# Every step of a four-layer attention kernel placed anew, with plans and PSUM banks of their own for the first two and the last two groups

## Chip, cores and metric

The kernel runs on one core of one Trainium2 chip. The metric is the device time of one launch in microseconds, the median of three runs.

## What is computed

A batch of 128 sequences, 64 tokens of 128 features, goes through four layers, each of which also reads a context tensor of the same shape. In short:

```python
x = L0(x, ctx)   # 16 heads of 8: q/k/v projections, causal scores (key < query), softmax, Wo,
                 # + x, layernorm, relu FFN 128-512-128, + , layernorm
x = L1(x, ctx)   # 16 heads of 8, no mask, softmax(q k / sqrt(8)) v, Wo, + x, gelu FFN, +
x = L2(x, ctx)   # vision = mean over ctx tokens; agreement with the text projection gives a softmax
                 # over tokens; gate = sigmoid(...); x + gate * weighted vision; layernorm
x = L3(x, ctx)   # RMS norm, 16 heads of 64: softmax(q k) v, wo, + x
```

No sequence depends on another one.

## The kernel before

The batch is cut into 16 groups of 8 sequences (512 tokens). For each group the kernel does the same 129 steps on TensorE (PE), and others on ScalarE (ACT), VectorE (DVE) and GpSimd (POOL). A step is a few instructions that belong together. The names that count here, with the layer l, the half u of a group, and the tile t:

- `xT`, `cT` transpose the input and the context; `q`, `k`, `v` project; `S.l.u` makes the scores of four sequences for layers 0 and 1, `shift.l.u.t` subtracts the row maximum in PSUM, `PT.l.u.t` transposes the probabilities, `O.l.u` multiplies them by the values, `o.l` is the output projection. Between them stand `max`, `sum`, `ctx`, `attout` on DVE, `exp`, `probT` on ACT, and `norm` on POOL (L895), which divides by the sum.
- `lnT.n`, `lnF.n` are the transposes into and out of a layernorm, with `stats` and `z` on DVE and `rstd` on POOL between; `h.l.j`, `f.l.j` are the FFN, with `relu` or `gelu` on ACT between.
- `vis`, `gv`, `ag`, `gp` belong to layer 2, with `amax`, `gate_pre`, `vis_route`, `fuse` on DVE, `route`, `gate` on ACT.
- `k3.p`, `v3.b`, `q3.p` project for layer 3 (three matmuls each), evicted on ACT as `K3`, `V3`, `Q3`; `rows` spreads the RMS factors; `S3.m`, `shift3`, `PT3`, `O3.m`, `out3.m` are its attention in four pairs of sequences, with `norm3` on POOL (L915).

`S`, `O`, `S3` and `O3` are the tiled steps: they use parts of the array (32x64, 64x32, 64x64 rows by columns), and each is 64 short matmul records with a weight load each; `S.0.u` has 16 more for the causal mask.

The order is written out by hand. `PLAN` (L52) gives for each engine the steps of one group and a time for each; `program()` (L141) adds `START[g]` (L112), sorts, and so interleaves the groups: about three are in work at a time. The times only make the order; each engine then runs its list in sequence and waits for semaphores where it must. `START` has steps of 89.65. The DMA queue loads a group's input when the group before has been transposed.

`BANK` (L116) gives each tile one of the eight PSUM banks, the same in all groups. `occupants()` (L173) walks through PE's order and notes for each tile which one held the bank before it; `freed()` (L434) makes PE wait until that one has been read. So a new order or a new bank also makes other waits.

At the start GpSimd makes `w_low`, the low parts of the split weights of layer 3, before its first `norm` (L886); every `k3`, `v3`, `q3` of group 0 waits for it.

Of the kernel before, what the change touches and what calls it, by code (L numbers as in the profile page):

```python
# [36 lines left out]
for _n, _w in [("W1_0", 512), ("W2_0", 512), ("W1_1", 512), ("W2_1", 512), ("wo3", 1024)]:  # L37
# [16 lines left out]
        xT@0 cT@1.01 q.0@7.77 k.0@9.09 S.0.0@14.64 shift.0.0.0@17.91 shift.0.0.3@22.49 shift.0.0.2@22.71  # L54
        shift.0.0.1@24.44 v.0@54.53 PT.0.0.3@57.35 PT.0.0.2@59.56 PT.0.0.0@60.01 PT.0.0.1@61.32 S.0.1@61.4
        O.0.0@63.65 shift.0.1.0@63.99 shift.0.1.1@65.43 shift.0.1.3@65.65 shift.0.1.2@66.73 PT.0.1.0@70.11
        PT.0.1.3@74.28 v.1@74.97 PT.0.1.1@75.14 PT.0.1.2@75.59 O.0.1@76.5 o.0@80.86 lnT.0@83.62 vis@88.92
        lnF.0@89.17 gv@89.55 h.0.1@90.72 h.0.0@91.58 h.0.2@92.96 h.0.3@93.3 f.0.0@94.16 f.0.1@95.02
        f.0.2@96.33 f.0.3@97.19 lnT.1@99.61 k.1@102.94 lnF.1@106.56 q.1@109.17 S.1.0@115.13
        shift.1.0.2@117.16 shift.1.0.0@117.85 shift.1.0.1@119.75 shift.1.0.3@122.59 PT.1.0.2@122.75  # L60
        PT.1.0.0@124.23 PT.1.0.1@124.57 PT.1.0.3@126.18 O.1.0@128.18 S.1.1@130.32 shift.1.1.0@134.16
        shift.1.1.2@134.83 k3.2@135.28 shift.1.1.3@135.77 k3.1@136.85 shift.1.1.1@138.51 k3.4@140.38
        PT.1.1.2@141.27 PT.1.1.0@141.66 PT.1.1.1@142.56 PT.1.1.3@143.06 O.1.1@146.53 o.1@149.88 h.1.0@154.18
        h.1.1@155.48 h.1.2@156.56 h.1.3@157.42 k3.6@157.81 k3.5@158.57 f.1.0@160.17 f.1.1@161.03 f.1.2@161.89
        f.1.3@162.75 ag@165.69 gp@166.92 k3.0@169.46 v3.6@169.53 k3.3@171.11 k3.7@171.39 v3.1@171.62
        v3.5@173.69 v3.7@173.82 v3.3@175.4 v3.4@175.88 v3.0@176.25 lnT.2@177.67 v3.2@177.85 lnF.2@185.53
        q3.7@189.71 q3.5@190.43 q3.2@191.52 q3.3@191.87 q3.4@193.05 q3.0@193.87 q3.6@196.28 q3.1@197.35
        rows@198.99 S3.0@199.57 S3.1@200.61 shift3.0.0@201.73 shift3.0.1@202.57 shift3.1.0@203.15
        shift3.1.1@203.86 PT3.0.0@206.45 PT3.0.1@207.9 S3.2@208.46 O3.0@209.9 PT3.1.0@211.16 out3.0@212.65
        PT3.1.1@215.31 shift3.2.0@215.76 S3.3@216.56 shift3.2.1@217.69 shift3.3.0@218.96 O3.1@219.28  # L70
        shift3.3.1@221.66 out3.1@222.1 PT3.2.0@223.53 PT3.2.1@223.71 O3.2@226.06 PT3.3.1@226.84
        PT3.3.0@228.54 out3.2@228.99 O3.3@234.1 out3.3@236.9""",
    "ACT": """
        c_high@4.13 qm.0@9.8 exp.0.0.0@19.71 exp.0.0.2@24.7 exp.0.0.1@27.2 exp.0.0.3@31.06 probT.0.0.3@58.06
        probT.0.0.2@60.27 probT.0.0.0@61.27 probT.0.0.1@62.07 exp.0.1.0@64.36 exp.0.1.3@65.66 exp.0.1.1@66.26
        exp.0.1.2@67.16 probT.0.1.0@68.47 probT.0.1.3@74.99 probT.0.1.1@77.52 probT.0.1.2@77.89
        ln_out.0@90.28 relu.1@91.84 relu.0@92.7 relu.2@95.13 relu.3@95.3 ln_out.1@107.07 qm.1@110.63
        exp.1.0.2@118.37 exp.1.0.0@119.38 exp.1.0.1@120.23 exp.1.0.3@123.07 probT.1.0.2@124.27
        probT.1.0.0@125.09 probT.1.0.1@125.28 probT.1.0.3@127.08 exp.1.1.0@135.69 exp.1.1.2@136.29
        exp.1.1.3@136.89 exp.1.1.1@138.99 K3.1@139.1 K3.2@140.51 probT.1.1.2@142.13 probT.1.1.0@142.37  # L80
        probT.1.1.1@143.57 probT.1.1.3@144.22 K3.4@150.2 gelu@157.64 K3.5@163.06 K3.6@164.45 route@168.26
        V3.6@170.51 K3.0@171.76 K3.3@172.09 V3.1@172.36 gate@173.41 V3.7@174.09 K3.7@175.45 V3.5@175.76
        V3.0@177.23 V3.3@178.42 V3.4@178.78 V3.2@183.66 yn_high@187.08 square@187.77 Q3.7@189.86 Q3.5@191.41
        Q3.2@192.98 Q3.3@193.21 Q3.4@194.03 Q3.0@194.85 Q3.6@197.85 Q3.1@198.33 exp3.0.0@202.39
        exp3.0.1@203.34 exp3.1.0@204.27 exp3.1.1@205.61 prob3T.0.0@207.39 prob3T.0.1@208.61 ctx3.0.1@211.31
        ctx3.0.0@211.91 prob3T.1.0@213.51 prob3T.1.1@216.32 exp3.2.0@217.52 exp3.2.1@218.31 exp3.3.0@219.44
        ctx3.1.1@220.69 ctx3.1.0@221.29 exp3.3.1@222.14 prob3T.2.0@224.05 prob3T.2.1@224.23 ctx3.2.1@227.47
        ctx3.2.0@228.07 prob3T.3.1@229.43 prob3T.3.0@231.2 ctx3.3.0@235.51 ctx3.3.1@236.11""",
    "DVE": """
# [14 lines left out]
        norm.0.0.0@19.06 norm.0.0.2@36.61 norm.0.0.3@44.09 norm.0.0.1@53.45 norm.0.1.0@67.17 norm.0.1.3@68.23
        norm.0.1.1@70.31 norm.0.1.2@71.37 rstd.0@88.02 rstd.1@102.34 norm.1.0.2@120.41 norm.1.0.0@122.13
        norm.1.0.1@122.94 norm.1.0.3@125.06 norm.1.1.0@137.33 norm.1.1.2@138.94 norm.1.1.1@140.63
        norm.1.1.3@141.72 rstd.2@181.2 rms@193.29 norm3.0.0@205.33 norm3.0.1@206.39 norm3.1.0@207.18
        norm3.1.1@213.83 norm3.2.1@221.42 norm3.2.0@222.48 norm3.3.1@224.45 norm3.3.0@226.06""",
# [1134 lines left out]
```

## Time and profile before

| | us |
|---|---|
| median of 3 runs | 1546.05 (1545.48 to 1546.59) |
| the profiled execution, its own time | 1548.49 |
| its span, first to last instruction | 1546.8 |
| PE busy in the span | 1421.6 (92%) |
| DVE, ACT, POOL busy | 1079.5, 975.0, 489.8 |
| mean granted TensorE clock | 0.982 of full speed |

The page divides the span into 40 slices and gives the busy share of each engine in tenths:

```
PE   5679999999999999999999999899999999999877
DVE  4467768686786867778686877768687786866643
ACT  3246667666676766667676666667666676756554
PEclk9789999999999999999999999999999999999999
```

A row of the timeline is: start, duration, engine, line, operation, the tile that is written and those that are read, shape, count of merged instructions, and in brackets the idle time of that engine before it with the instruction that ended it. "<-issue" there means that the profile shows nothing for which the engine waited. Matmuls overlap, so the distance between two starts is shorter than the duration. A row of the windows gives for a stretch its length, the busy time of PE, PE's weight loads, DVE, ACT and POOL (with counts of instructions), the granted clock, the DMA share and the GB/s. A row of waits gives who waited for whom, the total, the number of times and the longest.

### The profile page before, as it was taken

The numbers are of one execution on the slowest core, as the hardware profiler recorded it, in microseconds if no ns is written. First come the engines' busy times: TensorE is split into PE (matmuls) and PEld (weight loads), VectorE is DVE, ScalarE is ACT, GpSimd is POOL, SyncE is SP. The second block draws the span as 40 slices with busy tenths as digits, with TensorE's granted clock in tenths as the row PEclk, the third lists the DMA queues.
The fourth block names the chain that finished last, engine by engine and source line by source line (L and its number), as shares of the span: only waits on it lengthen the run. The fifth ranks groups of instructions, "written<-read, shape, count | busy, mean of one in ns | idle before, by whom it ended". The sixth has DMA issues, their size and how long they took to land.

```text
span 1546.8 us, 53472 instructions
## 1 busy us (share of the span) xinstructions
PE 1421.6 (92%) x22629; PEld 1046.0 (68%) x22629; DVE 1079.5 (70%) x2644; ACT 975.0 (63%) x1877; POOL 489.8 (32%) x522
## 2 busy tenths in 40 slices
PE   5679999999999999999999999899999999999877
PEld 3446776767677676867667686676767677676655
DVE  4467768686786867778686877768687786866643
ACT  3246667666676766667676666667666676756554
POOL 2132423314252331525233151423315142331402
PEclk9789999999999999999999999999999999999999
DMA  4000000000000000000000000000000000000000
GB/s 140 14 1 15 3 9 16 9 16 10 15 3 9 16 10 15 10 15 3 9 16 9 16 10 15 3 8 16 10 15 3 22 3 9 2 10 1 3 8 9
DMA packets 27816, 20.31 MB, mean 13 GB/s; under 512 B 1088, under 2 KB 27200, under 8 KB 27328
## 3 DMA queue, kind: packets, MB, share of 16 engines
q1 hardware_dynamic: 27584, 16.90, 3.7%
q8 instruction: 185, 3.03, 0.8%
q14 instruction: 47, 0.39, 0.1%
HBM read 12.70 MB, written 4.19 MB: 11 GB/s over the span
## 4 chain that ended last, share of the span: by engine, by line
PE 83%; DVE 6%; issue 4%; POOL 3%; ACT 3%; DMA 0%; SPq 0%; ACTq 0%; DVEq 0%
PE bank L487 68%; PE bank L496 15%; DVE z L1075 2%; POOL rstd L902 2%; ACT prob L854 1%; DVE stats L1061 1%; DVE negmax L1017 1%; POOL var_eps L899 1%; POOL prob L895 1%; ACT prob L782 1%; POOL w_low L886 0%; DVE mv L1066 0%; ACT Q L867 0%; DMA vec<-in_vectors 0%; DVE sums L1022 0%
## 5 line engine op out<-in xcount | busy, mean ns | idle before, releaser
L895 POOL TENSOR_TENSOR prob<-prob,rinv 128x512 f32<-128x512 f32 x256 | 263.6, 1042 | 361.5 <-DVE rinv L1024 359.2
L496 PE MATMUL bank<-cst,prob 128*128 128x128 f32 x1536 | 217.8, 279 | 14.9 <-POOL prob L915 6.0
L496 PEld LDWEIGHTS bank<-cst,prob 128*128 128x128 f32 x1536 | 180.2, 143 | 54.9 <-issue 27.5
L789 ACT ACTIVATE probT<-bank 128x512 f32<-128x512 f32 x256 | 144.8, 600 | 92.2 <-PE bank L496 90.6
L782 ACT ACTIVATE prob<-bank 128x512 f32<-128x512 f32 x256 | 146.9, 604 | 82.0 <-PE bank L487 81.9
L1022 DVE TENSOR_REDUCE sums<-prob 128x8 f32<-128x512 f32 x256 | 171.0, 668 | 38.9 <-ACT prob L782 37.7
L1017 DVE TENSOR_REDUCE negmax<-bank 128x8 bf16<-128x512 f32 x256 | 162.9, 674 | 46.3 <-PE bank L487 45.7
L915 POOL TENSOR_TENSOR prob<-prob,rinv 128x512 f32<-128x512 f32 x128 | 132.0, 1042 | 198.5 <-DVE rinv L1168 198.1
L899 POOL TENSOR_TENSOR var_eps<-mv,ln_eps 128x4 f32<-128x4 f32 x48 | 14.9, 310 | 455.1 <-DVE mv L1066 455.1
L487 PE MATMUL bank<-negmax,ident_b 128*128 128x512 bf16 x384 | 134.9, 391 | 11.6 <-DVE negmax L1017 8.7
L854 ACT ACTIVATE prob<-bank,rms_rows 128x256 f32<-128x256 f32 x256 | 103.9, 482 | 64.6 <-PE bank L487 62.3
L487 PE MATMUL bank<-wt,Q 128*128 128x128 f32 x1024 | 126.6, 277 | 3.8 <-ACT Q L867 3.0
L487 PEld LDWEIGHTS bank<-wt,Q 128*128 128x128 f32 x1024 | 120.2, 192 | 7.0 <-ACT Q L867 3.0
L487 PE MATMUL bank<-room,wt 128*128 128x512 f32 x256 | 117.6, 592 | 0.0
L1036 DVE TENSOR_SCALAR half_ctx<-bank,cst,vec 128x126 f32<-128x126 f32 (+1 forms) x128 | 46.6, 403 | 91.4 <-PE bank L487 91.4
L837 ACT ACTIVATE V<-bank 128x512 f32<-128x512 f32 x128 | 73.1, 599 | 53.1 <-PE bank L487 53.0
L487 PE MATMUL bank<-room 32*64 32x128 f32 x4096 | 81.7, 285 | 24.5 <-ACT prob L782 11.9
L1158 DVE TENSOR_REDUCE negmax<-bank 128x8 bf16<-128x512 f32 x128 | 81.0, 675 | 32.5 <-PE bank L487 32.5
L862 ACT ACTIVATE prob3T<-bank 128x512 f32<-128x512 f32 x128 | 75.8, 606 | 40.7 <-PE bank L496 40.7
L1164 DVE TENSOR_REDUCE sums<-prob 128x8 f32<-128x512 f32 x128 | 85.6, 669 | 16.2 <-ACT prob L854 15.0
L487 PE MATMUL bank<-c_high,w_high 128*128 128x512 f32 x160 | 95.3, 596 | 1.6 <-ACT K L832 1.2
L487 PE MATMUL bank<-probT,Vm 64*32 64x128 f32 x4096 | 79.5, 275 | 18.3 <-issue 15.4
(155 smaller groups left out, 2953.3 us busy)
## 6 DMA issues: line engine op xcount, KB each, us to landing
x_in<-in_x SPq DMA_DIRECT2D x16, 256.0 KB, 3.0
...
```

Of the source, the lines that this page charges most:

```text
L487: return nc.tensor.matmul(o, lhsT, rhs, start=start, stop=stop, skip_group_check=True)
L496: last = nc.tensor.transpose(o[:, k * P:(k + 1) * P], src(k), ident)
L782: nc.scalar.activation(prob[l][:, t].rearrange("p c k -> p (c k)"), bank("S", l, u, t)[:, :], ACT.Exp, scale=SCALE8).then_inc(exp_ready.se ...
L789: nc.scalar.activation(probT[:, t].rearrange("p s q -> p (s q)"), bank("PT", l, u, t)[:, :], ACT.Identity).then_inc(probT_ready.sem, 1)
L854: last = nc.scalar.activation(prob3[:, m % 2, :, i, :].rearrange("p (t e) k -> p t e k", e=2)[:, :, e, :], bank("S3", m, e)[:, 256 * i:256 ...
L862: nc.scalar.activation(prob3T[:, 4 * h:4 * h + 4, :].rearrange("p j q -> p (j q)"), bank("PT3", m, h)[:, :], ACT.Identity).then_inc(prob3T ...
L895: nc.gpsimd.tensor_tensor(pr, pr, ri, ALU.mult).then_inc(norm_ready.sem, 1)
L915: nc.gpsimd.tensor_tensor(pr, pr, ri, ALU.mult).then_inc(norm3_ready.sem, 1)
L1017: nc.vector.tensor_reduce(negmax[l][:, t, :], bank("S", l, u, t)[:, :].rearrange("p (c k) -> p c k", c=8), AX.X, ALU.max, negate=True).the ...
L1022: nc.vector.tensor_reduce(sums[l][:, t, :], prob[l][:, t], AX.X, ALU.add).then_inc(sum_ready.sem, 1)
L1158: nc.vector.tensor_reduce(negmax3[:, m % 2, e, :], bank("S3", m, e)[:, :].rearrange("p (c k) -> p c k", c=8), AX.X, ALU.max, negate=True). ...
L1164: nc.vector.tensor_reduce(sums3[:, m % 2, 4 * h:4 * h + 4].rearrange("p j i -> p (j i)"), prob3[:, m % 2, 4 * h:4 * h + 4].rearrange("p j ...
```

## The change

Nothing is computed otherwise, and no instruction of any step is altered; each step gets another place in the order of its engine, and each tile another bank.

- `PLAN` is written anew for the groups 2 to 13, and `PLANS` holds four more plans, for groups 0, 1, 14 and 15. `program()` adds `TURN * g` instead of `START[g]`; `AHEAD`, which moved `K3` and `V3` a little in two groups, goes away.
- `BANKS` holds five lists of banks, one for each plan; `bank()` takes the group as its first argument, and every use of it in the steps is changed so (some 60 places, all alike).

```diff
-START = [0, 89.64, 179.32, 268.97, 358.62, 448.27, 537.92, 627.57, 717.22, 806.87, 896.52, 986.17, 1075.82, 1165.47, 1255.13, 1344.76]
+TURN = 89.7521
...
+def plan_of(group):
+
+    return {0: 0, 1: 1, G - 2: 3, G - 1: 4}.get(group, 2)
...
-    plan = [parse(token) for token in PLAN[engine].split()]
-    placed = [(START[g] + at - AHEAD.get((kind, g), 0.0), kind, index, g) for g in range(G) for kind, index, at in plan]
+    placed = [(TURN * g + at, kind, index, g) for g in range(G)
+              for kind, index, at in map(parse, PLANS[plan_of(g)][engine].split())]
...
-        def bank(kind, *tile):
-            return psum[BANK[".".join([kind, *map(str, tile)])]]
+        def bank(group, kind, *tile):
+            return psum[BANK[plan_of(group)][".".join([kind, *map(str, tile)])]]
```

What the sorted plans come to, for the part of PE's order with most tiled steps, from S.0.0 of group 8 on (`/8` is the group; the same in all middle groups). Before:

```
S.0.0/8 lnF.1/7 q3.6/6 shift.0.0.0/8 q3.1/6 q.1/7 rows/6 S3.0/6 S3.1/6 shift3.0.0/6 shift.0.0.3/8
shift.0.0.2/8 shift3.0.1/6 shift3.1.0/6 shift.0.0.1/8 shift3.1.1/6 S.1.0/7 PT3.0.0/6 shift.1.0.2/7
shift.1.0.0/7 PT3.0.1/6 S3.2/6 shift.1.0.1/7 O3.0/6 PT3.1.0/6 shift.1.0.3/7 PT.1.0.2/7 out3.0/6
PT.1.0.0/7 PT.1.0.1/7 PT3.1.1/6 shift3.2.0/6 PT.1.0.3/7 S3.3/6 shift3.2.1/6 O.1.0/7 shift3.3.0/6
O3.1/6 S.1.1/7 shift3.3.1/6 out3.1/6 PT3.2.0/6 PT3.2.1/6 shift.1.1.0/7 shift.1.1.2/7 k3.2/7
shift.1.1.3/7 O3.2/6 k3.1/7 PT3.3.1/6 shift.1.1.1/7 PT3.3.0/6 out3.2/6 k3.4/7 PT.1.1.2/7
PT.1.1.0/7 PT.1.1.1/7 PT.1.1.3/7 v.0/8 O3.3/6 O.1.1/7 PT.0.0.3/8 out3.3/6
```

After:

```
S.0.0/8 lnF.1/7 q3.7/6 q3.5/6 rows/6 q.1/7 S3.0/6 shift.0.0.3/8 k.1/7 shift3.0.0/6 shift.0.0.0/8
shift.0.0.1/8 shift3.0.1/6 S3.1/6 shift.0.0.2/8 S.1.0/7 shift3.1.1/6 PT3.0.0/6 shift3.1.0/6
PT3.0.1/6 shift.1.0.0/7 shift.1.0.2/7 S3.2/6 O3.0/6 shift.1.0.1/7 shift.1.0.3/7 PT3.1.0/6
shift3.2.0/6 PT3.1.1/6 shift3.2.1/6 S3.3/6 out3.0/6 PT.1.0.3/7 shift3.3.0/6 O3.1/6 PT.1.0.0/7
PT.1.0.1/7 PT.1.0.2/7 shift3.3.1/6 PT3.2.0/6 O.1.0/7 S.1.1/7 PT3.2.1/6 k3.1/7 shift.1.1.1/7
O3.2/6 shift.1.1.3/7 shift.1.1.0/7 shift.1.1.2/7 out3.1/6 PT.1.1.1/7 out3.2/6 PT.1.1.0/7
PT.1.1.3/7 k3.2/7 PT.1.1.2/7 PT3.3.0/6 PT3.3.1/6 O.1.1/7 PT.0.0.1/8 O3.3/6 o.1/7 v.1/8 ...
```

Group 0 begins on PE with `xT cT q.0 k.0 S.0.0` before, and with `xT cT q.0 k.0 vis k3.2 S.0.0` after; between `lnT.0` and `lnF.0` it has `vis` before, and `xT/1 k3.0 cT/1 k3.6 k.1` after; `S.1.1` stands before `O.1.0` after. In group 15, `lnT.2 v3.2 lnF.2 q3.7` becomes `lnT.2 k3.4 v3.3 v3.0 k3.7 lnF.2 k3.6 v3.7 q3.2`, the order of `h.1` becomes 3, 0, 1, 2, and the end `out3.2 O3.3 out3.3` becomes `O3.3 out3.2 out3.3`. On POOL, `rstd.0/8 rstd.2/7 rstd.1/8 rms/7` becomes `rstd.0/8 rstd.2/7 rms/7 rstd.1/8`.

## Rows read from the trace of the kernel before

**Rows 1.** The page: busy time of the engines, and the largest group of instructions.

```profile
PE 1421.6 (92%) x22629; PEld 1046.0 (68%) x22629; DVE 1079.5 (70%) x2644; ACT 975.0 (63%) x1877; POOL 489.8 (32%) x522
...
L895 POOL TENSOR_TENSOR prob<-prob,rinv 128x512 f32<-128x512 f32 x256 | 263.6, 1042 | 361.5 <-DVE rinv L1024 359.2
```

**Rows 2.** Windows: start, middle and end of the span, and one period.

```profile
0.00:154.80 154.80, 113.04 (x1200) 74.83 (x1200) 90.85 (x249) 66.30 (x114) 39.77 (x46) 0.88 0.14 43
154.80:1333.30 1178.50, 1128.33 (x18391) 835.76 (x18391) 871.22 (x2121) 786.28 (x1522) 392.76 (x416) 1.00 0.04 11
1333.30:1546.80 213.50, 180.27 (x3048) 135.43 (x3047) 117.39 (x277) 122.41 (x242) 57.30 (x60) 0.96 0.02 6
...
970.80:1063.00 92.20, 86.74 (x1423) 64.31 (x1423) 67.18 (x165) 60.62 (x118) 30.20 (x32) 1.00 0.04 11
```

**Rows 3.** Waits of PE from 154.8 to 1333.3 us.

```profile
PE bank L487 <- issue: 24.4, 46, 1.3
PE bank L487 <- ACT prob L782: 11.1, 13, 1.1
PE bank L496 <- DVE z L1075: 5.5, 13, 0.4
```

**Rows 4.** Timeline of PE: tiled steps, with and without a hole.

```profile
836.91 1.16 PE L487 MATMUL bank<-room 32*64 32x128 f32 x64
838.04 1.15 PE L487 MATMUL bank<-probT,Vm 64*32 64x128 f32 x64
839.12 0.39 PE L487 MATMUL bank<-negmax,ident_b 128*128 128x512 bf16 x1
...
540.10 0.67 PE L487 MATMUL bank<-probT,Vm 64*32 64x128 f32 x32
541.87 0.67 PE L487 MATMUL bank<-probT,Vm 64*32 64x128 f32 x32 [1.10 <-issue]
542.48 0.39 PE L487 MATMUL bank<-negmax,ident_b 128*128 128x512 bf16 x1
...
545.47 0.87 PE L487 MATMUL bank<-room 32*64 32x128 f32 x36 [0.63 <-issue]
...
179.53 0.38 PE L487 MATMUL bank<-probT,Vm 64*32 64x128 f32 x2 [1.20 <-issue]
...
1268.41 0.69 PE L487 MATMUL bank<-prob3T,V 64*64 64x64 f32 x30 [0.26 <-issue]
```

**Rows 5.** The page, DMA queues: packets, MB, share of 16 engines.

```profile
q8 instruction: 185, 3.03, 0.8%
```

**Rows 6.** Timeline of PE: from S3.0 to PT3.0.0.

```profile
884.70 2.09 PE L487 MATMUL bank<-K,Q 64*64 64x64 f32 x128 [0.26 <-issue]
...
889.62 1.20 PE L487 MATMUL bank<-room 32*64 32x128 f32 x64 [0.81 <-ACT prob L782]
891.08 0.63 PE L496 MATMUL bank<-cst,prob 128*128 128x128 f32 x4 [0.26 <-POOL prob L915]
```

**Rows 7.** Timeline, first 34 us: S.0.0, w_low and the first transposes.

```profile
18.64 0.65 PE L487 MATMUL bank<-causal_rows,causal_pick 32*64 32x256 bf16 x16 [1.62 <-DVE room L999]
...
19.95 6.69 POOL L886 TENSOR_TENSOR w_low<-Q,w_high 128x3072 fp32r<-128x3072 f32 x1 [18.88 <-ACT w_high L778]
...
29.79 3.65 PE L496 MATMUL bank<-cst,prob 128*128 128x128 f32 x16 [4.33 <-POOL prob L895]
```

**Rows 8.** From 1333.3 us on: PE's waits, and timeline around lnF.2 and q3.

```profile
PE bank L487 <- issue: 8.4, 10, 1.5
...
1498.79 0.63 PE L496 MATMUL bank<-cst,z 128*128 128x128 f32 x4 [3.68 <-DVE z L1075]
1501.80 0.76 PE L487 MATMUL bank<-yn_high,w_high 128*128 128x512 f32 x1 [2.38 <-DVE yn_low L1140]
1502.37 0.63 PE L487 MATMUL bank<-yn_low,w_high 128*128 128x512 f32 x1
1502.79 0.63 PE L487 MATMUL bank<-yn_high,w_low 128*128 128x512 f32 x1
```

More of the change, by code:

```diff
@@ L53 @@
     "PE": """
[L54 to L72, printed above, removed]
-    "ACT": """
[L74 to L88, printed above, removed]
@@ L103 @@
-    "POOL": """
[L104 to L108, printed above, removed]
-}
@@ new lines @@
+        v3.4@498.2541 v3.6@499.2964 v3.3@501.0457 k3.0@501.627 k3.6@501.6807 k3.3@502.2278 v3.0@502.4578 v3.7@503.4343
+        lnT.2@503.9044 lnF.2@511.7578 q3.2@516.0274 q3.6@516.9318 q3.3@519.1754 q3.0@519.6628 q3.1@519.7888 q3.4@520.7886
+        q3.7@523.7917 q3.5@524.6579 rows@524.9672 S3.0@525.7332 shift3.0.0@526.8302 shift3.0.1@528.8122 S3.1@528.9016
+        shift3.1.1@532.5578 PT3.0.0@533.0614 shift3.1.0@533.2775 PT3.0.1@533.38 S3.2@535.615 O3.0@535.9968 PT3.1.0@538.0246
+        shift3.2.0@538.1307 PT3.1.1@538.4787 shift3.2.1@540.2104 S3.3@541.1685 out3.0@541.2979 shift3.3.0@542.6991
@@ new lines @@
+    "POOL": """
+        norm.0.0.2@370.8193 norm.0.0.1@380.0403 norm.0.0.3@384.9605 norm.0.0.0@392.9761 norm.0.1.2@396.813 norm.0.1.0@407.939
+        norm.0.1.3@409.3346 norm.0.1.1@410.495 rstd.0@416.6818 rstd.1@424.7038 norm.1.0.0@438.7573 norm.1.0.3@440.6895
+        norm.1.0.2@447.5254 norm.1.0.1@449.8038 norm.1.1.1@463.2848 norm.1.1.0@464.9067 norm.1.1.3@465.2816
+        norm.1.1.2@467.1569 rstd.2@509.335 rms@510.4439 norm3.0.0@516.2505 norm3.0.1@518.488 norm3.1.0@521.161
+        norm3.1.1@522.1231 norm3.2.0@549.2434 norm3.2.1@551.7345 norm3.3.0@553.0758 norm3.3.1@559.5063""",
+}
@@ new lines @@
+TILES = """
+        xT cT vis gv q.0 k.0 v.0 v.1 S.0.0.0 S.0.0.1 S.0.0.2 S.0.0.3 PT.0.0.0 PT.0.0.1 PT.0.0.2 PT.0.0.3 O.0.0.0 O.0.0.1
+        S.0.1.0 S.0.1.1 S.0.1.2 S.0.1.3 PT.0.1.0 PT.0.1.1 PT.0.1.2 PT.0.1.3 O.0.1.0 O.0.1.1 o.0 lnT.0 lnF.0 h.0.0 h.0.1 h.0.2
+        h.0.3 f.0 lnT.1 lnF.1 q.1 k.1 S.1.0.0 S.1.0.1 S.1.0.2 S.1.0.3 PT.1.0.0 PT.1.0.1 PT.1.0.2 PT.1.0.3 O.1.0.0 O.1.0.1
+        S.1.1.0 S.1.1.1 S.1.1.2 S.1.1.3 PT.1.1.0 PT.1.1.1 PT.1.1.2 PT.1.1.3 O.1.1.0 O.1.1.1 o.1 h.1.0 h.1.1 h.1.2 h.1.3 f.1
+        gp ag lnT.2 lnF.2 rows k3.0 k3.1 k3.2 k3.3 k3.4 k3.5 k3.6 k3.7 v3.0 v3.1 v3.2 v3.3 v3.4 v3.5 v3.6 v3.7 q3.0 q3.1 q3.2
+        q3.3 q3.4 q3.5 q3.6 q3.7 S3.0.0 S3.0.1 PT3.0.0 PT3.0.1 O3.0.0 O3.0.1 S3.1.0 S3.1.1 PT3.1.0 PT3.1.1 O3.1.0 O3.1.1
+        S3.2.0 S3.2.1 PT3.2.0 PT3.2.1 O3.2.0 O3.2.1 S3.3.0 S3.3.1 PT3.3.0 PT3.3.1 O3.3.0 O3.3.1 out3"""
@@ L177, in occupants @@
     tiles = {}
-    for name, bank in BANK.items():
+    for name in TILES.split():
         kind, *index = name.split(".")
-        tiles.setdefault(kind, []).append((tuple(int(i) for i in index), bank))
+        tiles.setdefault(kind, []).append((tuple(int(i) for i in index), name))
     for kind, index, group in PROGRAM["PE"]:
-        for tile, bank in tiles.get(kind, []):
-            n = min(len(tile), len(index))
+        for tile, name in tiles.get(kind, []):
+            n, bank = min(len(tile), len(index)), BANK[plan_of(group)][name]
             if tile[:n] == index[:n] and not any(index[n:]):
@@ L539, in step @@
                     pe.wait_ge(*c_low_ready(g))
-                    o = bank("v", u)
+                    o = bank(g, "v", u)
                     for i in range(2):
@@ L655, in step @@
                     pair = slice(b // 2 * P, b // 2 * P + P)
-                    split_mm(bank("v3", b)[:, :], [part[:, pair] for part in context],
+                    split_mm(bank(g, "v3", b)[:, :], [part[:, pair] for part in context],
                              w_split("wv3", b % 2 * TOK, TOK)).then_inc(v3_filled.sem, 1)
@@ L726, in step @@
                     for p in range(PAIRS):
-                        last = mm(bank("out3")[:, k * P:(k + 1) * P],
+                        last = mm(bank(g, "out3")[:, k * P:(k + 1) * P],
                                   Q3[:, p, 2 * k:2 * k + 2, :].rearrange("p b q -> p (b q)"),
@@ L1060, in step @@
                     for k in range(CH):
-                        last = nc.vector.bn_stats(stats[l][:, k, :], bank("lnT", n)[:, k * P:(k + 1) * P])
+                        last = nc.vector.bn_stats(stats[l][:, k, :], bank(g, "lnT", n)[:, k * P:(k + 1) * P])
                     last.then_inc(stats_ready.sem, 1)
```

421 lines of the change are left out of this document (347 added, 74 removed), and 15 rows, old and new, of the table BANK.

## Prediction

> **What bounds the kernel now.** I read the page first: TensorE (PE) is busy for 92% of the span, the next engine 70% [rows 1]. So the time is PE's work plus PE's idle time, and I cut the span where PE's order shows a seam: before S.0.0 of group 2 (154.8 us) and of group 15 (1333.3 us) [rows 2]. Between them stand 13 periods, 1178.5 us, so 90.65 each, of which PE is busy for 1128.3/13 = 86.8; they differ (one of them is shown, with 92.2) although every period has the same steps and nearly the same busy time. The start takes 154.8 us with 113.0 busy, the end 213.5 with 180.3.
>
> Next the waits of PE in the middle [rows 3]. The largest entry has no producer: "issue", 24.4 us in 46 waits. The next are 11.1 for an exp (S.1.0 waits for a bank) and 5.5 for z of the layernorm.
>
> The timeline says where "issue" lies [rows 4]. A tiled step (S, O, S3, O3) is 64 short matmuls with 64 weight loads, done in about 1.1 us: O.0.0 starts at 838.04 and the next step at 839.12. O.1.0 at 540.10 stops halfway, goes on at 541.87 and ends for its successor at 542.48: 2.38 us instead of 1.08, 1.30 more for an idle time of 1.10. I went through all periods so: 26 such holes stand inside tiled steps, the first at 179.53, the last at 1268.41, with 18.2 us idle; with 0.25 each of lost overlap that is 24.7 us, 1.9 per period. All of them are in a step that follows another tiled step with at most one shift between. By place: 17 in the run S3.3, O.1.0, O3.1, S.1.1 (10.5 idle, so 14.7 us or 1.13 per period), 4 in O.0.0 behind S.0.1 (5.05 us, 0.39), 3 in O.1.1 behind O3.3 (3.45 us, 0.27), one each in S3.1 and O3.0 (0.07 and 0.04). What is short of supply is instructions. The page has 185 packets of kind "instruction" on one queue, 3.03 MB [rows 5], so 16.4 KB each; PE has 45,258 matmuls and weight loads, 245 for each packet. A pair of adjacent tiled steps eats a packet's worth in 2.2 us, a period as a whole takes 7.8 us for one. At 541.87 and 545.47 two holes follow each other after 3.6 us, which I take as the time of one packet when PE outruns the supply.
>
> Here a rule of the Trainium skill is weighed. Its page "Runtime: NRT & Kernel Launch", section "Instruction fetch mechanics", says that instructions come in blocks of 256 and that crossing into a new one is "mostly hidden". The count of packets agrees; "hidden" doesn't hold next to a hole of 1.10 us. By the page, spacing the tiled steps would be worth nothing, and the middle would stay at 1178.5 us but for the waits.
>
> **The change, part by part.**
>
> *Order of the middle periods.* The same 129 steps, no instruction added. In the new order the run of four is gone: S3.3, O3.1 and O.1.0 each have about 2 us of other PE work ahead of them. Five pairs stay or arise: S.0.1/O.0.0 as before (0.39), O.1.1/O3.3 with one transpose step between (0.27 as now), and O.1.0/S.1.1, S3.2/O3.0, and S3.1/S.1.0 with a shift between. A pair's price is between the cheapest and the dearest pair of the trace, 0.04 and 0.39; I take 0.25 for O.1.0/S.1.1, which lies in denser work, 0.10 for each of the other two. Sum 1.11 instead of 1.90: 0.79 less per period; with the bounds, 0.07 to 1.12 less.
>
> *Waits in the middle.* (a) From S3.0 to the first transpose of its probs, PE waits for exp, sum and norm: S3.0 starts at 884.70, PT3.0.0 at 891.08, with 0.81, 0.26 and small gaps between, 1.2 in all [rows 6]. The new order puts k.1 (0.7 us) there and takes one shift more behind it, with the chain of the same length: 0.3 less. (b) lnT.0 to lnF.0 goes through statistics, rstd and z; PE waits 5.5/13 = 0.4 for it now. The work between goes from 4.9 to 4.6 us: 0.3 more. (c) shift.1.1.x to PT.1.1.x: now 3.7 to 6.8 us of PE work lie between, then 3.4 to 5.4, and norm3.3.0 enters GpSimd's queue between norm.1.1.1 and norm.1.1.0. A norm takes 1.04 us [rows 1], four tiles and that one 5.2 us, against some 4.6 us of work from PT.1.1.1 to PT.1.1.2 plus what is ahead: between 0 and 0.6, I take 0.1, near the zero that this place shows now. (d) The rest of the chains (scores to shift, prob to O, O to o, f to layernorm) keep distances at least as long as places that show no wait today. (e) In GpSimd's order rms of the group before now stands ahead of rstd.1, which waits behind it; rms's input is ready some 2 us earlier than that of rstd.1, so nothing. Together +0.1, with bounds of -0.5 and +0.9.
>
> So a period is worth -0.69 us, 13 of them -9.0 (bounds -21 and +11).
>
> Mode changes of the array are a second rule against: "TensorEngine Tiling (Array Packing)", section "Key Properties", says that changing the tiling mode drains the engine. The rows show S.0.1 of one mode and O.0.0 of another 1.13 us apart, no more than the step's own length, and the order has 28 changes instead of 27: by rule or row this is at most 0.1 us per period.
>
> *The start.* New is k3.2 of group 0 ahead of S.0.0. It needs w_low, which GpSimd makes from 19.95 to 26.64 [rows 7]; with its three matmuls S.0.0 starts near 28.0 instead of 18.64. Not all of that counts, since norm.0.0.x has to queue behind w_low now as well: PT waits until 29.79. After: 28.0 + 3.1 to the first shift + 1.0 (exp) + 0.9 (sum) + 1.04 (norm) = 34.1 for the first transpose and 1.04 per tile after, S.0.1 near 38.7 instead of 33.4, where the transposes end now: +5.3. What pays it back: gv and O.0.0 go into the wait for the norms (-0.8); xT, cT of group 1 and k3.0, k3.6, k.1 fill the 4.09 us before lnF.0, so that h.0 comes 0.4 us sooner; v3.2, v3.5 fill the next one; S.1.1 of group 0 goes ahead of O.1.0 and no longer waits behind it (-2). By O.1.1 of group 0, PE has 3.4 us more work behind it, and from there on it is bound by work. 5.3 - 0.8 - 0.4 - 2 - 3.4 = -1.3; I take 0, since each filler can push the chain, with bounds of -5 and +6.
>
> *The end.* Holes: 8.4 us of "issue" in 10 waits [rows 8]; in the two groups' own plans the run of four is broken too: -2. Chain of group 15: PE idles 3.68 us before lnF.2 and 2.38 before q3, and then runs 11 of q3's matmuls at half the granted clock, 0.42 us apart instead of 0.23, 2.3 us lost [rows 8]. Four steps now stand in the first gap, where one did, and k3.6, v3.7 in the second, so the clock may stay; but ScalarE has four more evictions of 0.6 us ahead of Q3's, so S3.0 gains 1.5 and not 2.3. From ag to lnT.2 PE had 7.8 us of work for a chain of about the same length; half of it is moved away, -0.5. h.1.3 ahead of h.1.0 delays gelu by 0.9. out3.2 behind O3.3 fills its eviction, -0.5. Sum -3.6; I take -4 with the other fillers, bounds -9 and +3.
>
> Sum: -9.0 + 0 - 4.0 = -13.0 us. The profiled span is 1546.8 (1548.5 with what lies around it), the median of the three runs 1546.05; I take the difference off the median: 1533.0 us. A measurement of this kernel tells about 0.2% from no change, 3.1 us: 1543.0 and 1549.1 are the borders.
>
> **The rivals.**
>
> 1. *The gain is eaten.* The holes leave, but the time comes back as waits for norms and z: where PE is faster by 0.8, the chains of (a) to (c) end last. For it: 24.4 us of holes stand beside 11.1 and 5.5 us of true waits [rows 3], so both limits are near each other. Against: work of two other groups lies between most links. It gives 13 x 0 - 4 + 4 = 0: 1546.
>
> 2. *Slower: norms bind.* GpSimd's queue is in order, so one late sum holds every norm behind it; PT.1.1.x, PT.0.0.x and with them O and the next group's start slip. Its price is one or two norms, 1.04 to 2.08 us, per period; from 0.8 us on it is dearer than the holes. With 1.6 per period and the start's +4: 13 x (1.6 - 0.8) + 4 - 4 = +10: 1556. For it: GpSimd's distances shrink in (c). Against: it is busy for 32% only.
>
> 3. *The spacing does not do what it says.* If the holes come wherever a packet ends, pairs are as bad as the run of four: 1.8 per period remain. Then 13 x (-0.1 + 0.1) - 3 = -3: 1543, on the border of no change; it's the case that the Runtime page's "hidden" would lead to also, by other means.
>
> 4. *More than forecast.* Pairs at 0.04 and the end at its bound: 13 x (-1.1) - 8 = -22: 1524.
>
> **Chances.** Forecast 0.64, rival 1 0.08, rival 2 0.12, rival 3 0.06, rival 4 0.10. Faster: 0.64 + 0.10 + half of rival 3 and a little of rival 1 = 0.78; same: 0.10; slower 0.12. The range reaches from below rival 4, 1517, to 1547, which takes in rivals 1 and 3 and leaves out rival 2 and a few per cent below.
>
> **What would show it.** Right: "issue" in the middle near 14 us instead of 24.4, no hole in O3.1, periods near 90.0; w_low's end followed by k3.2 and S.0.0 of group 0 near 28; waits for z near 9 us in the middle. Wrong: "issue" unchanged (rival 3), or L895/L915 as the first waits of PE with more than 10 us (rivals 1 and 2), or S.0.0 of group 2 later than 161.

## The result, and the profile after

The changed kernel took 1537.14 us (median of 5 runs, 1533.91 to 1539.23) beside 1546.05 (1542.65 to 1548.29) of the kernel before: ratio 0.9944, 95% interval 0.9926 to 0.9961, so 8.7 us or 0.56% faster, 4.1 us above the forecast. The profiled execution has a span of 1535.6 us against 1546.8. From the page, to be read beside [rows 1] and [rows 5], and the windows cut at the same steps as in [rows 2] (S.0.0 of group 2 is at 154.50 now, that of group 15 at 1337.94):

```profile
PE 1425.8 (93%) x22629; PEld 1034.3 (67%) x22629; DVE 1081.0 (70%) x2644; ACT 976.8 (64%) x1877; POOL 488.8 (32%) x522
PEclk8799999999999999999999999999999999999999
q8 instruction: 185, 3.03, 0.8%
```

```profile
0.00:154.50 154.50, 112.98 (x1202) 73.76 (x1202) 90.56 (x248) 64.62 (x114) 39.85 (x46) 0.88 0.15 43
154.50:1337.90 1183.40, 1135.37 (x18380) 829.68 (x18379) 873.17 (x2121) 790.45 (x1521) 391.92 (x416) 1.00 0.04 11
1337.90:1535.60 197.70, 177.41 (x3051) 130.90 (x3050) 117.27 (x278) 121.72 (x243) 57.03 (x60) 0.99 0.02 6
```

| stretch | before | after | difference | forecast |
|---|---|---|---|---|
| start | 154.8 | 154.5 | -0.3 | 0 |
| 13 periods | 1178.5 | 1183.4 | +4.9 | -9.0 |
| end | 213.5 | 197.7 | -15.8 | -4.0 |

The total came out near the forecast by luck: two errors, 13.9 us in the middle and 11.8 at the end, cancel. The middle, where most of the gain was expected, is slower; the end gained four times its estimate. The waits of PE in the middle, beside [rows 3]:

```profile
PE bank L731 <- issue: 17.2, 25, 1.6
PE bank L740 <- DVE z L1319: 7.1, 13, 0.6
PE bank L740 <- POOL prob L1159: 6.6, 29, 0.4
PE bank L731 <- ACT probT L1033: 4.5, 13, 0.5
...
PE bank L740 <- issue: 1.8, 2, 1.1
```

"issue" fell from 24.4 to 19.0 us. The exp that S.1.0 waited for (11.1 us in [rows 3]) is all but gone. New are 4.5 us for probT ahead of O.1.0, and the norms went from 3.4 us in 12 waits to 6.6 in 29. Idle time in the middle fell from 50.2 to 48.0 us (length less busy), but busy time rose by 7.0 with the same work. Modelled ends hide a part of a wait in the matmul ahead of it, so I compare distances between the starts of steps, not idle time alone.

In the timeline O3.1 of group 4 now stands behind S3.3, out3.0 and a shift, and runs through; in the run of [rows 4] it stood between O.1.0 and S.1.1. O3.0, which follows S3.2 directly, stops instead:

```profile
537.24 1.16 PE L731 MATMUL bank<-K,Q 64*64 64x64 f32 x64
538.34 2.05 PE L731 MATMUL bank<-wt,Q 128*128 128x128 f32 x16
...
540.97 1.16 PE L731 MATMUL bank<-prob3T,V 64*64 64x64 f32 x64
...
442.44 1.16 PE L731 MATMUL bank<-K,Q 64*64 64x64 f32 x64 [0.20 <-ACT prob L1098]
443.51 0.59 PE L731 MATMUL bank<-prob3T,V 64*64 64x64 f32 x25
445.18 0.81 PE L731 MATMUL bank<-prob3T,V 64*64 64x64 f32 x39 [1.08 <-issue]
```

Counted as in the forecast, 15 holes stand inside tiled steps of the middle instead of 26, with 14.6 us idle instead of 18.2: four in O3.0, four in O3.3, three in S.1.0, two each in O.0.0 and S.1.1. 13 of them are over 0.3 us (19 before). Three stops more stand just behind a tiled step and not inside it, 0.6 us at 716.88, 1.1 at 819.91 and 1.5 at 1211.47 (the last one is booked as a wait for negmax), 3.3 us together. The trace before has 2.2 us in three such stops (817.19, 979.13, 1285.63), so the step from 18.2 to 14.6 us flatters the new order a little.

The theory that I took to the chip: a hole depends on where the instruction count stands. I counted PE's matmuls, weight loads and waits in the trace. A period has 2959 of them in both kernels, and every hole inside a tiled step stands at one and the same remainder of that count modulo 256 (between the same two neighbours of the count, of which one is a weight load and one a matmul). 2959 leaves 143 over, so the place moves from period to period and the holes with it. A fit to both traces says that a hole mostly comes where the last 212 or so instructions ahead of such a place run in under 2.7 us. It is an estimate and a rough one: e4 below has such a place in O.0.0, where these instructions take 1.9 us, and no hole comes.

The instruction packets in the traces tie the holes to supply. PE's queue is the one with the 185 packets: 45,258 matmuls and weight loads and 2,097 waits make 185 times 256. Ahead of each of the 208 holes over 0.3 us that the 14 traces of this case have inside tiled steps, a packet of this queue starts 2.1 to 3.1 us before PE goes on, and ends 1.2 to 1.6 us before it. For the hole at 445.18 the figures are 2.4 and 1.5 us.

### The profile page after: what moved, and what is told of

It reads as the page before. It is cut to its first block, busy times and chain, and to the rows that moved or that the text cites. A ratio compares the mean times of both kernels' runs of the same rounds, so it can differ in the third digit from the quotient of the medians.

```text
span 1535.6 us, 53473 instructions
## 1 busy us (share of the span) xinstructions
PE 1425.8 (93%) x22629; PEld 1034.3 (67%) x22629; DVE 1081.0 (70%) x2644; ACT 976.8 (64%) x1877; POOL 488.8 (32%) x522
## 4 chain that ended last, share of the span: by engine, by line
PE 76%; DVE 10%; ACT 5%; POOL 4%; issue 4%; DMA 0%; SPq 0%; ACTq 0%; DVEq 0%
PE bank L731 63%; PE bank L740 13%; DVE negmax L1261 2%; ACT prob L1098 2%; POOL prob L1159 2%; POOL rstd L1146 1%; DVE sums L1408 1%; DVE z L1319 1%; ACT probT L1033 1%; DVE negmax L1402 1%; DVE stats L1305 1%; POOL var_eps L1143 1%; POOL w_low L1130 0%; POOL prob L1139 0%; DVE mv L1310 0%
## 5 line engine op out<-in xcount | busy, mean ns | idle before, releaser
L740 PE MATMUL bank<-cst,prob 128*128 128x128 f32 x1536 | 222.1, 279 | 13.8 <-POOL prob L1159 7.8
L740 PEld LDWEIGHTS bank<-cst,prob 128*128 128x128 f32 x1536 | 175.9, 142 | 60.3 <-issue 34.2
L1261 DVE TENSOR_REDUCE negmax<-bank 128x8 bf16<-128x512 f32 x256 | 159.0, 680 | 75.8 <-PE bank L731 75.8
L1026 ACT ACTIVATE prob<-bank 128x512 f32<-128x512 f32 x256 | 141.9, 608 | 85.1 <-PE bank L731 84.9
L731 PE MATMUL bank<-negmax,ident_b 128*128 128x512 bf16 x384 | 128.4, 386 | 14.9 <-DVE negmax L1261 9.5
L731 PE MATMUL bank<-room,wt 128*128 128x512 f32 x256 | 123.3, 593 | 0.0
L1076 ACT ACTIVATE K<-bank 128x512 f32<-128x512 f32 x128 | 74.1, 604 | 53.0 <-PE bank L731 52.7
L1402 DVE TENSOR_REDUCE negmax<-bank 128x8 bf16<-128x512 f32 x128 | 81.4, 658 | 29.5 <-PE bank L731 29.4
L1111 ACT ACTIVATE Q<-bank 128x512 f32<-128x512 f32 x128 | 71.7, 596 | 45.5 <-PE bank L731 45.5
L731 PE MATMUL bank<-c_high,w_high 128*128 128x512 f32 x160 | 86.2, 539 | 10.6 <-POOL w_low L1130 9.4
```

The source lines that it names most:

```text
L731: return nc.tensor.matmul(o, lhsT, rhs, start=start, stop=stop, skip_group_check=True)
L740: last = nc.tensor.transpose(o[:, k * P:(k + 1) * P], src(k), ident)
L1026: nc.scalar.activation(prob[l][:, t].rearrange("p c k -> p (c k)"), bank(g, "S", l, u, t)[:, :], ACT.Exp, scale=SCALE8).then_inc(exp_ready ...
L1261: nc.vector.tensor_reduce(negmax[l][:, t, :], bank(g, "S", l, u, t)[:, :].rearrange("p (c k) -> p c k", c=8), AX.X, ALU.max, negate=True). ...
L1402: nc.vector.tensor_reduce(negmax3[:, m % 2, e, :], bank(g, "S3", m, e)[:, :].rearrange("p (c k) -> p c k", c=8), AX.X, ALU.max, negate=Tru ...
```

## Experiments

Each was timed in 5 rounds, with the kernel before on the same chip. Ratios are to that kernel, brackets hold the 95% interval.

| kernel | us | before beside it | ratio |
|---|---|---|---|
| e1 old order, new end | 1533.1 | 1542.9 | 0.9936 [0.9921, 0.9951] |
| e2 new order, old end | 1544.0 | 1542.9 | 1.0010 [0.9996, 1.0024] |
| e3 changed, 57 extra matmuls, 10 at the start | 1515.5 | 1542.9 | 0.9829 [0.9810, 0.9848] |
| e4 the same, 54 at the start | 1530.7 | 1542.9 | 0.9914 [0.9896, 0.9932] |
| e5 before, 57 extra matmuls | 1547.8 | 1545.2 | 1.0014 [1.0000, 1.0027] |
| e6 as e5, new end | 1538.2 | 1545.2 | 0.9958 [0.9942, 0.9973] |
| e7 changed, steady plan at the end | 1543.5 | 1545.2 | 0.9984 [0.9970, 0.9997] |
| e8 changed, again | 1530.7 | 1545.2 | 0.9916 [0.9893, 0.9939] |
| e9 changed, k3.2 of group 0 later | 1525.3 | 1545.2 | 0.9868 [0.9851, 0.9884] |
| e11 changed, waits merged | 1511.7 | 1545.2 | 0.9782 [0.9768, 0.9797] |
| e10 waits merged, 76 extra matmuls | 1507.9 | 1545.2 | 0.9759 [0.9745, 0.9774] |
| e12 e10 and e9 | 1502.7 | 1543.9 | 0.9722 [0.9702, 0.9743] |

**Where the gain is: e1 and e2.** Both orders stand in one kernel, with one cut ahead of S.0.0 of group 14 (shortened):

```
    early = [s[1:] for s in sorted(FIRST(engine)) if s[0] < CUT]
    late = [s[1:] for s in sorted(SECOND(engine)) if s[1:] not in early]
    return early + late
```

> Every engine follows the order and the banks of the kernel before up to the place just ahead of S.0.0 of group 14, and from there on the changed kernel's order and banks: start and middle are old, the end is new. Theory E (the gain stands in the last two groups; the traces have 213.5 us behind S.0.0 of group 15 before and 197.7 after, and the middle 178.5 against 1183.4 for the 13 periods' 1178.5 before): 12 to 16 us faster than the kernel before, 1530 to 1534 us, so that it also beats the changed kernel. Theory F, as forecast (middle -9, end -4): 1542 us. If the seam costs something, up to 2 us more in either case.

> The reverse: the changed kernel's order and banks up to the place just ahead of S.0.0 of group 14, the order and banks of the kernel before from there on: start and middle are new, the end is old. Theory E (middle and start together 4 to 5 us slower than before, the gain is in the end): 1550 us. Theory F, as forecast (middle -9, start 0): 1537 us.

(In the first text the middle before is 1178.5 us; the "178.5" is a slip.) The windows of e1, then of e2 (length, PE busy, clock, DMA share, GB/s):

```profile
0.00:152.00 152.00, 111.39 (x1200) 0.92 0.15 43
152.00:1330.20 1178.20, 1128.43 (x18380) 1.00 0.04 11
1330.20:1529.20 199.00, 177.60 (x3051) 0.99 0.02 6
...
0.00:148.50 148.50, 107.21 (x1200) 0.98 0.16 44
148.50:1328.20 1179.70, 1134.92 (x18383) 1.00 0.04 11
1328.20:1541.00 212.80, 179.78 (x3048) 0.96 0.02 6
```

The new end alone gives 0.64% (9.9 us); the new start and middle give nothing that can be measured (+0.10%, slower if anything; the interval holds zero). e1 gained 9.9 us where theory E had 12 to 16, and e2 lost 1.0 where it had 4 to 5 (its start took 148.5 us, not 154.5); both are far from theory F. So the gain of this change that can be placed is in the last two groups: 0.9936 times 1.0010 is 0.9946, beside 0.9944 of the first measurement. (The second one, e8, has 0.9916; the 0.3% between are not placed by these runs.) How much slower the new middle is: it took 1183.4, 1182.2, 1179.7, 1178.3 and 1179.9 us in the five traces that have it, the old one 1178.5 and 1178.2. That is 0 to 5 us, 2 in the mean, and no gain in any of them.

**What a hole is: e3, e4, e8, e5, e6.** Extra matmuls stand in a wait that is there anyway, and their output is overwritten (shortened):

```
+  if n == 0 and g >= 3:                     # lnF.0
+      for i in range(57):
+          rows = slice(32 * (i % 4), 32 * (i % 4) + 32)
+          mm(bank(g, "lnF", 0)[rows, 0:32], causal_pick[rows, 0, 0:32], causal_rows[rows, :])
```

e3 has 10 more (fp32, of ident) between cT and q.0 of group 0, e4 has 54.

> The changed kernel with 57 small extra matmuls (their result is overwritten by the step itself) ahead of lnF.0 of each group from the third steady one on, in the place where TensorE waits 0.7 us for z, and 10 at the start between cT and q.0 of group 0. They make the instructions of a period 3072 instead of 2959, which is 12 times 256, so that the places where TensorE stood without work in the trace (all at one residue modulo 256 of its instruction count) fall on the same steps in every period; with 10 at the start none of them falls near a tiled step that follows a tiled step. Supply theory (a hole comes where some 212 instructions ahead of such a place run in less than 2.7 us): holes 0 to 0.2 us per period instead of 1.5, the pads cost 0.2: periods of 89.5 instead of 91.0, total 1520 to 1526 us. Rival (the holes have another cause, the place in the count does not matter): the same dozen holes and 3 us more for the pads, 1540 us.

> As the one ahead, but with 54 instead of 10 extra matmuls at the start, which shifts the places by 176 instructions (80 backwards modulo 256). Supply theory: a hole of about 1.1 us in O3.0 and one of about 0.9 us in O.0.0 (behind S.0.1) in every period from group 3 on, and none elsewhere in the middle: 2.0 us per period, periods of 91.3, total 1540 to 1545 us, about 20 us more than with 10 although the work of the periods is the same. Rival: within 3 us of it.

e3, windows (the middle, one period) and PE's waits from 239.4 to 1223 us; then two of the holes of e4 in its timeline:

```profile
239.40:1223.00 983.60, 964.17 (x16198) 1.00 0.04 11
776.11:865.51 89.40, 87.75 (x1472) 1.00 0.04 11
...
PE bank L731 <- ACT probT L1042: 3.8, 11, 0.4
PE bank L731 <- issue: 0.9, 3, 0.4
```

```profile
709.36 0.33 PE L731 MATMUL bank<-prob3T,V 64*64 64x64 f32 x4 [0.71 <-issue]
...
799.71 0.33 PE L731 MATMUL bank<-prob3T,V 64*64 64x64 f32 x4 [1.26 <-issue]
```

In e3 no hole over 0.3 us is left in a tiled step between groups 2 and 12, and from group 4 to 13 a period takes 89.24 to 89.50 us, where the changed kernel's vary from 90.0 to 92.9. In e4 every period has its hole in O3.0, 60 matmuls in, and takes 89.8 to 90.4 us. The work of a period is the same; only the place in the count differs, and the medians are 15.2 us apart (the two traces 11.7, of which the periods make 10; the executions of e4 also have the lower mean clock, 0.986 to 0.992 against 0.992 to 0.997). The rival, that the place does not matter, is out. The size was off: the expected second hole, in O.0.0, does not come, so that e4 was 9 us below its range; e3 was 5 us below its own, of which 3 are this chip, where the kernel before takes 1542.9.

> The changed kernel once more, for its time and trace beside the three others on one chip. The ratio to before should be 0.9944 again (0.9926 to 0.9961); the holes should stand in the same steps of the same groups if they hang on the instruction count, and in others if they are chance.

All 13 holes over 0.3 us in the middle came again in the same steps of the same groups; a fourteenth, in S.1.0 of group 11, had 0.25 us after and 0.5 now. For example O3.0 of group 3, 25 matmuls in, as at 445.18 above:

```profile
444.00 0.81 PE L731 MATMUL bank<-prob3T,V 64*64 64x64 f32 x39 [1.49 <-issue]
```

Their place is fixed by the program, their length is not (1.08 and 1.49 us). The ratio, 0.9916, is below the first one's interval, but the two intervals overlap.

Could the old order have had this without any spacing? In e5 the extra matmuls stand ahead of S.1.0, where PE waits for the exp; e6 adds the new end.

> The kernel before in its own order and banks, with 57 small extra matmuls per group (overwritten by the step itself) ahead of S.1.0, in the 0.9 us where TensorE waits there for an exp, and 15 at the start between cT and q.0 of group 0. A period has then 3072 = 12 x 256 instructions, and the places at which TensorE can run short fall on the same steps in every period, away from the second half of the pairs. No step is spaced. Supply theory: one hole of about 0.4 us in S.1.1 per period or none, periods of 88.6 to 88.9 instead of 90.6, so 22 us less in the middle: 1518 to 1525 us. Rival S (tiled steps next to each other cost holes by themselves, whatever the count says; only spacing them, as the change does, takes them away): the run of four still has its holes, periods of 90.5 or more, 1541 us or above.

> The same pads in the kernel of e1 (old order up to group 14, new order and banks behind it). If the two gains are independent: e5 less the 10 us that e1 measured for the new end, 1508 to 1516 us, faster than every kernel so far. If the end's gain was in truth the absence of holes in the last two groups (its instructions stand elsewhere in the count now, and holes may come back there), 1516 to 1522.

e5, timeline of the run of four in one period, and its waits from 242 to 1246 us:

```profile
722.71 0.67 PE L487 MATMUL bank<-probT,Vm 64*32 64x128 f32 x32 [1.39 <-issue]
...
725.00 0.68 PE L487 MATMUL bank<-room 32*64 32x128 f32 x28 [0.21 <-DVE aT L1050]
726.87 0.87 PE L487 MATMUL bank<-room 32*64 32x128 f32 x36 [1.19 <-issue]
```

```profile
PE bank L487 <- issue: 27.1, 33, 1.4
```

My expectation failed: the time is the one that rival S named. The places do stand fixed now: from group 1 to 14 each period has one hole in O.1.0 and one in S.1.1, 3.6 to 4.2 us apart. Together they are 2.2 us idle per period, where the kernel before has 1.4 in all.

But e5 doesn't show that the old order has no better place, because the place it fixes is one of the dearest. O.1.0 stops 32 matmuls in and S.1.1 28 in, just as in the period of [rows 4], which took 91.6 us (517.0 to 608.6). In the period ahead of that one the same run of four stands elsewhere in the count. It took 89.2 us in the trace before and 88.7 in that of e1, whose middle has the same order. Here is e1, the period and its run of four from O.1.0 to S.1.1:

```profile
424.98:513.68 88.70, 86.42 (x1415) 64.28 (x1414) 66.93 (x164) 60.48 (x118) 30.19 (x32) 1.00 0.04 11
...
447.18 1.16 PE L829 MATMUL bank<-probT,Vm 64*32 64x128 f32 x64
448.27 0.39 PE L829 MATMUL bank<-negmax,ident_b 128*128 128x512 bf16 x1
448.59 0.80 PE L829 MATMUL bank<-prob3T,V 64*64 64x64 f32 x37
449.65 0.68 PE L829 MATMUL bank<-prob3T,V 64*64 64x64 f32 x27 [0.27 <-issue]
450.26 1.21 PE L829 MATMUL bank<-room 32*64 32x128 f32 x64
```

With one hole of 0.27 us in four dense steps, this period is as short as any of e10 below. My fit, with the distance to the place before added, gives the old order 1.5 us per period at best, and that at e5's place (an estimate); it doesn't hold, since the trace of e5 has 2.2 us idle there and this one 0.27 at another place. No run fixed the old order at its cheap place. So e3 and e4 show what the place is worth, but whether the spaced order is needed for that gain stays open. Without a fixed place, either order has as many holes as its dense steps happen to meet.

e6 is 0.56% faster than e5, of the 0.64% that the new end gave alone: the extra matmuls and the new end don't disturb each other.

**The end: e7.** What runs differs in one line: plan_of gives the steady plan to groups 14 and 15. That takes away their own banks and all of their own order, the fillers with it.

> The changed kernel without plans of their own for the last two groups: they follow the steady plan and its banks, so that the tiled steps are set apart as in the change, but nothing fills TensorE's waits between lnT.2, lnF.2 and q3 of the last group. Theory E1 (the end's gain came from spacing and from where the instructions fall): 1 to 3 us slower than the changed kernel. Theory E2 (it came from the fillers: gaps of 3.7 and 2.4 us before, now 0.9 and 1.0, and q3 no longer at half clock): 6 to 9 us slower than the changed kernel.

e7: windows of the end, and PE's waits in it:

```profile
1327.70:1538.80 211.10, 181.94 (x3051) 0.95 0.02 6
...
PE bank L801 <- DVE z L1380: 4.9, 2, 4.4
PE bank L792 <- DVE yn_low L1445: 2.4, 1, 2.4
PE bank L792 <- issue: 2.4, 4, 1.5
```

The end takes 211.1 us, near the 213.5 before, although the tiled steps are set apart; with own plans 197.7 to 200.6 (after, e1, e8, e9). In time e7 is 0.7% slower than e8 and 0.4% slower than the first measurement of the changed kernel: 6 to 11 us. That is theory E2: the end's gain comes from the plans of its own, not from the spacing. That it is the fillers is read from the waits, which are back (4.4 us for z, 2.4 for yn_low, and a clock of 0.95 instead of 0.99); no run took the fillers away alone.

**The start: e9.** In group 0's plan k3.2@328.1104 becomes k3.2@419.1 (behind k3.6), K3.2@361.2956 becomes K3.2@426.7.

> The changed kernel with k3.2 of group 0 taken away from ahead of S.0.0 of group 0: it stands behind k3.6 now, its eviction behind that of k3.6. S.0.0 of group 0 no longer waits for w_low: near 18.5 us instead of 27.7. Forecast of the start (the delay of S.0.0 is paid back, since the norms have to queue behind w_low anyway): the same time as the changed kernel within 2 us, and S.0.0 of group 1 at the same place within 2 us. Rival (the delay of S.0.0 costs its 5 us, and other moves of the start hide it): 3 to 5 us faster than the changed kernel.

In the changed kernel the chain was as forecast, k3.2 directly behind w_low and S.0.0 behind it at 27.74:

```profile
19.46 6.65 POOL L1130 TENSOR_TENSOR w_low<-Q,w_high 128x3072 fp32r<-128x3072 f32 x1 [18.38 <-ACT w_high L1022]
...
26.16 0.80 PE L731 MATMUL bank<-c_high,w_high 128*128 128x512 f32 x1 [9.41 <-POOL w_low L1130]
...
27.74 0.65 PE L731 MATMUL bank<-causal_rows,causal_pick 32*64 32x256 bf16 x16
```

In e9 S.0.0 starts at 17.1, S.0.0 of group 1 at 70.5 and that of group 2 at 147.0, where the eight other traces with the new start have 148.5 to 154.5. e9 is 0.5 to 0.8% faster than the changed kernel; e12 against e10 gives 0.37%, 5.7 us. The delay is not paid back: the rival was right, and its 3 to 5 us were too few. Part of the start is the granted clock: from 30 to 100 us it was 0.82 in the profiled execution after and 0.95 in e2, and the seam came at 154.5 and 148.5. The six executions of e8 show the same: 1528 to 1531 us at a mean clock of 0.995 to 0.997, 1536 and 1539 at 0.986 to 0.989.

**What the middle's new constant time is: e10 and e11.** A period's fastest course had grown too. Where waits follow each other in the trace, most stand 0.105 to 0.126 us apart (0.106 ahead of S3.0), and many are doubled: S3.0 waits for each of eight K3 and eight Q3 by the same two semaphores. Merged (shortened):

```
+  def wait_ge(signal, value):
+      held[id(signal)] = (signal, max(value, held.get(id(signal), (signal, 0))[1]))
+  def flush():                               # ahead of each matmul
+      for signal, value in held.values():
+          engine.wait_ge(signal, value)
+      held.clear()
```

> The changed kernel with merged waits alone, no extra matmul. Theory W: 2 to 8 us faster than the changed kernel; a period has 2921 instructions, so that the holes go on wandering, about 1 us per period. Rival: the changed kernel's time within 2 us.

> The changed kernel, TensorE's waits merged: where several waits on one semaphore stand ahead of an instruction, only the one for the largest value is left, 38 instructions per period less (each takes 0.105 us where they follow each other in the trace, as ahead of S3.0), and 76 instead of 57 extra matmuls per group, 28 at the start, so that a period has 3072 instructions again and the model has no hole in it. Theory W (the new constant idle time ahead of S3.0 and O.1.0, 0.45 and 0.50 us per period, is partly these wait instructions): 2 to 7 us less than e3, ratio to before 0.978 to 0.981, although the pads cost 0.3 more per period. Rival (they wait for Q3 and probT themselves): the time of e3 plus 3 us, 0.985.

q.1 and S3.0 in the timeline, after and in e11, and the waits of e11 from 243 to 1234 us:

```profile
794.60 1.10 PE L731 MATMUL bank<-fT,wt 128*128 128x512 f32 x2
795.83 1.16 PE L731 MATMUL bank<-K,Q 64*64 64x64 f32 x64
...
778.34 1.10 PE L744 MATMUL bank<-fT,wt 128*128 128x512 f32 x2
779.38 1.16 PE L744 MATMUL bank<-K,Q 64*64 64x64 f32 x64
...
PE bank L754 <- POOL prob L1174: 8.2, 35, 0.8
PE bank L744 <- issue: 6.3, 8, 1.4
PE bank L754 <- DVE z L1334: 6.2, 11, 0.6
```

S3.0 comes 1.04 us behind q.1 instead of 1.23 to 1.40 (median 1.31), O.1.0 and O.0.1 0.20 sooner each and O.0.0 0.18 (medians over the periods). The fastest periods take 88.6 us; e3's, which have no hole either, 89.3. "issue" falls from 17.2 (15.4 and 1.8) in the same periods to 6.3, so the holes went down too; whether fewer instructions or a lucky place did that, e11 alone doesn't tell. e10 against e3, both without such holes in these periods, is the cleaner pair: 0.9759 to 0.9829, so 0.7%. The gain over the changed kernel is 1.3 to 1.6% (by e8's ratio or the first), two to three times theory W's upper end of 8 us. In e10 nine periods follow each other with 88.69 to 88.72 us each:

```profile
240.70:1217.10 976.40, 962.50 (x16399) 703.74 (x16399) 737.46 (x1795) 668.83 (x1287) 330.87 (x352) 1.00 0.04 11
```

**All together: e12.**

> e9 and e10 together: merged waits, 76 extra matmuls per group and 28 at the start, and k3.2 of group 0 behind k3.6. If the start's part is independent of the rest, the ratio to before is 0.9759 less the 0.006 that e9 gained over the changed kernel: 0.970, 1498 to 1503 us on a chip where before takes 1545, with the same periods of 88.7 us. Rival (k3.2's place gains only beside the other moves of the start, or moves the granted clock): 0.976, as e10.

1502.7 us, 2.8% faster than the kernel before and 2.0 to 2.2% faster than the changed one by the ratios. The periods are e10's. The start's part is 0.0037, between the two expectations.

## Why the prediction was right and wrong, point by point

- **Bound (right).** PE's work and its idle time set the end, and the largest idle entry was instruction supply. e3 against e4 shows it: between them only the place changes, by 44 small matmuls at the start, and S.0.0 of group 0 moves by no more than 0.3 us.
- **Holes of the middle (direction right, size off by a third).** Left were 14.6 us idle and 0.25 for each of the 15 holes, 18.4 in all, so 1.41 per period instead of the forecast 1.11, a saving of 0.49 and not 0.79. The mis-sized term is the pairs: S3.2/O3.0, taken at 0.10, costs (4.8 + 1.0)/13 = 0.45; O.1.1/O3.3 0.36 for 0.27; S.0.1/O.0.0 0.17 for 0.39; O.1.0/S.1.1 0.27 for 0.25; S3.1/S.1.0 0.17 for 0.10. A price per pair was the wrong unit: a pair costs nothing or one to two us, by its place in the count. The old order's 0.39 and 0.04 were samples of 13. Even the run of four has a place where it costs 0.27 idle (e1). No hole in O3.1: right.
- **Waits of the middle (wrong; this step cost the gain).** Forecast +0.1 per period; measured 4.9/13 + 0.49 = +0.87 (about 0.7 with the mean of the five middles, 2 us slower instead of 4.9). (b) z was right: 0.42 to 0.71 us. (a) failed: the distances around PT3.0.0, PT3.0.1 and PT3.1.0 have 1.7 us over the steps' own length, 1.0 before; I looked only at the first transpose, and the norms behind it bind one by one (29 waits). (d) failed at O.1.0, from nothing to 0.50, and at S3.0, from 0.18 to 0.45; it also overlooked 0.67 of gain, the exp ahead of S.1.0. I read distances in engine work and did not count wait instructions: behind short steps these are late themselves, and merging them gave back 0.7 (e11, e3).
- **Start (delay right, payment wrong).** S.0.0 at 27.74, as forecast (28.0). "It is paid back" failed: 0.37% (e12 against e10) to 0.8% (e9). It did not show in the start's sum, -0.3 us for a forecast of 0, since the rest of the new start gains about as much. Which of the fillers do so was not separated.
- **End (sign right, four times too small).** "Issue" there fell from 8.4 us in 10 waits [rows 8] to 0.3 (3.0 in e8), not by 2. The chain was under-priced most; its term left out that the filled gaps themselves get shorter:

```profile
PE bank L740 <- DVE z L1319: 0.9, 1, 0.9
...
1496.45 0.47 PE L731 MATMUL bank<-yn_high,w_high 128*128 128x512 f32 x1 [0.99 <-DVE yn_low L1384]
1496.76 0.39 PE L731 MATMUL bank<-yn_low,w_high 128*128 128x512 f32 x1
1496.99 0.39 PE L731 MATMUL bank<-yn_high,w_low 128*128 128x512 f32 x1
...
1503.36 0.82 PE L731 MATMUL bank<-K,Q 64*64 64x64 f32 x41 [0.92 <-ACT Q L1090]
```

  Against [rows 8], the waits of 3.68 and 2.38 us are 0.9 and 1.0, and q3 runs 0.23 us apart from its second matmul on, not 0.42: 2.8 + 1.4 + 2.3 = 6.5 us where I took 1.5. I had let ScalarE's four evictions eat the clock's part; the wait for Q is 0.9 us. And the last stretch, S3.0 to out3.3 of group 15, fell from 30.1 to 26.6 us, where I had 0.5.
- **Signs.** "Issue" in the middle is 19.0 us where 14 was named, a period takes 91.0 for 90.0, z 7.1 for 9; S.0.0 of group 0 and O3.1 came as named. By its signs for the middle the forecast was half met, which the total hides. Changes of mode showed no price: O.1.0 and S.1.1, of two modes, start 1.07 us apart (816.49 and 817.56), a tiled step's own length.
- **Chances.** Rival 1 (the holes leave, the time comes back as waits) is what the middle did, though probT, Q3 and the wait instructions took part beside norms and z. I gave it 0.08. Rival 2's single mechanism, a norm's length per period, did not come: norms cost 6.6 us in all. Rival 3 did not hold for O3.1, but its core did, that the places of the supply do not care for spacing.
- **The rule of the Trainium skill.** In 14 traces 208 holes over 0.3 us stand inside tiled steps, all at the same remainder modulo 256. That agrees with the blocks of 256 of the Trainium skill, page "Runtime: NRT & Kernel Launch", section "Instruction fetch mechanics". Its "mostly hidden" holds for slow stretches only: of e4's 12 places per period eleven leave no hole over 0.3 us in a tiled step, and the twelfth costs 0.7 to 1.3 us every time.
